# Reordering the attention heads of a three-stage layer: projections one step sooner, score products placed between attend products, batch loops written out

## What is computed

```
x = x + tanh(g0) * experts(layernorm(x), token_ids)       # 4 gated experts, each token one of them
h0 = layernorm(x)
a  = rmsnorm(h0, ln1)                                      # attention, 16 heads of width 32
q, k, v = a @ Wq.T, a @ Wk.T, a @ Wv.T
probs = softmax(mask_causal(q k^T / sqrt(32)))             # 512 x 512 for each head
mod = 0.1 * tanh(((probs v) @ Wo.T) @ A)                   # A is 512 x 16: only rank 16 of attention is used
h  = rmsnorm(h0, ln2)
gate = silu(h @ W_in.T + mod * (h @ A) @ B)
x = x + tanh(g1) * (h0 + (gate * (h @ W_up.T)) @ W_down.T) # 16 chunks of 128 of 2048
```

## Time and profile before

| | |
|---|---|
| median of 3 runs | 1061.95 us (1060.31 to 1062.95) |
| profiled execution | 1061.96 us |
| its span | 1059.8 us |
| PE busy | 1033.5 us, 98% |
| PEld busy | 853.5 us, 81% |
| DVE busy | 722.4 us, 68% |
| ACT busy | 589.6 us, 56% |
| POOL busy | 252.1 us, 24% |
| chain that ended last | PE 86%, DVE 8%, issue 3%, DMA 1%, ACT 1% |

### The profile page before, as it was taken

The page is one execution under the profiler, slowest core; times in us unless marked ns, Lnnn a source line. Parts: engine busy times, 40 slices in busy tenths (PEclk is TensorE's granted clock), DMA queues, the critical chain, the costliest instruction groups (busy, mean ns, idle before and its releaser), DMA issues.

```text
span 1059.8 us, 17623 instructions
## 1 busy us (share of the span) xinstructions
PE 1033.5 (98%) x5336; PEld 853.5 (81%) x5337; DVE 722.4 (68%) x1661; ACT 589.6 (56%) x1399; POOL 252.1 (24%) x252
## 2 busy tenths in 40 slices
PE   6999999999999999999999999999999999999998
PEld 6787878877888878878888888778888888788887
DVE  7766756996665559985665479966655599854443
ACT  4464546886434447875444368864344478753342
POOL 4536123641000115640000136410001155300000
PEclk9999999999999999999999999999999999999999
DMA  6534133443222416343322354432234253322221
GB/s 239 201 141 161 49 117 74 96 110 134 90 89 91 147 47 173 69 127 129 106 90 89 111 141 98 113 130 90 89 91 147 63 157 80 95 86 89 89 89 50
DMA packets 47084, 115.93 MB, mean 109 GB/s; under 512 B 6800, under 2 KB 6800, under 8 KB 46096
## 3 DMA queue, kind: packets, MB, share of 16 engines
q1 hardware_dynamic: 43968, 105.06, 33.2%
q0 software_dynamic: 3040, 9.96, 2.7%
HBM read 76.46 MB, written 13.37 MB: 85 GB/s over the span
## 4 chain that ended last, share of the span: by engine, by line
PE 86%; DVE 8%; issue 3%; DMA 1%; ACT 1%; SPq 0%; DVEq 0%; POOL 0%; POOLq 0%
PE bank L518 67%; PE bank L721 5%; PE bank L735 4%; DVE wr L1329 3%; PE bank L684 3%; DVE nb L1341 2%; PE bank L688 1%; PE bank L770 1%; DMA stack<-wr 1%; PE bank L574 1%; PE bank L589 1%; DVE big L1350 1%; PE bank L632 1%; SPq L312 0%; ACT wr L887 0%
## 5 line engine op out<-in xcount | busy, mean ns | idle before, releaser
L518 PE MATMUL bank<-hT,wr 128*128 128x512 f32 x1488 | 358.4, 390 | 0.0
L518 PEld LDWEIGHTS bank<-hT,wr 128*128 128x128 f32 x1488 | 278.8, 188 | 60.0 <-issue 1.3
L518 PE MATMUL bank<-wr,actr 128*128 128x512 f32 (+1 forms) x1224 | 303.1, 397 | 2.4 <-DVE actr L1311 1.5
L518 PEld LDWEIGHTS bank<-wr,actr 128*128 128x128 f32 x1224 | 228.8, 190 | 51.1 <-issue 3.3
L491 POOL TENSOR_SCALAR big<-big,rr 128x128 f32<-128x128 f32 (+1 forms) x128 | 138.9, 1094 | 131.7 <-DVE rr L1346 131.2
L1380 DVE SCALAR_TENSOR_TENSOR wr<-stream,lns,wr 128x256 fp32r<-128x256 f32 x256 | 121.7, 536 | 51.0 <-ACT wr L1006 51.0
L972 ACT ACTIVATE big<-bank,nb 128x512 f32<-128x512 f32 (+3 forms) x256 | 131.7, 527 | 27.9 <-DVE nb L1341 27.7
L430 POOL TENSOR_TENSOR wqs<-wstage,wqs 128x512 fp32r<-128x512 f32 x32 | 43.0, 1353 | 436.8 <-ACT wqs L887 435.4
L1329 DVE TENSOR_TENSOR wr<-bank,wr 128x512 fp32r<-128x512 f32 (+1 forms) x224 | 124.5, 600 | 22.2 <-ACT wr L887 22.2
L887 ACT ACTIVATE wr<-bank 128x512 fp32r<-128x512 f32 (+1 forms) x224 | 106.0, 538 | 52.9 <-PE bank L518 30.1
L887 ACT ACTIVATE actr<-act_sb 128x512 fp32r<-128x512 f32 x64 | 40.4, 632 | 145.7 <-DVE act_sb L1394 145.7
(11 more groups left out here) (180 smaller groups left out, 1039.6 us busy)
## 6 DMA issues: line engine op xcount, KB each, us to landing
stream<-in_wmlp SPq DMA_DIRECT2D x64, 512.0 KB, 4.0
stack<-wr SPq DMA_DIRECT2D x192, 128.0 KB, 2.3
stream<-in_wmlp SPq DMA_DIRECT2D x64, 256.0 KB, 2.7
big<-in_x SPq DMA_DIRECT2D x4, 1024.0 KB
big<-y_rows SPq DMA_DIRECT2D x4, 1024.0 KB, 5.5
residual<-big SPq DMA_DIRECT2D x4, 1024.0 KB
big<-residual SPq DMA_DIRECT2D x4, 1024.0 KB, 5.6
out<-big SPq DMA_DIRECT2D x3, 1024.0 KB, 4.5
```

The costliest lines, as they stand in the source:

```text
L518: mm = pe.matmul(dst, lhs(pl, k), rhs(pr, k), start=start and i == 0, stop=stop and i == n - 1, skip_group_check=skip)
```

## The change

On PE, the step of head `n` is now: turn of `n+1` in one run, the score rows of tiles 2 and 0 of head `n+3`, and then attend products of head `n` with the other short products between them; then half a projection for the step after, the two MLP products (from step 9), the last score row of head `n+4`, and the last attend product. The values are waited for ahead of the turn. Projections of groups 2 and 3 are done in the lead-in (one half) and in steps 0 to 6; all of group 1's K is in the lead-in. The tiles are turned in the order 2, 1, 3, 0, and the banks copied in the order 6, 5, 4. Normalising tile 0 goes to ACT, tile 1 to POOL. The product with zeros is gone. PE's and SP's loop over the batches is written out, that of ACT and DVE stays. SP has one more wait at the first head of groups 1 to 3; POOL makes the weights of group 2's Q in the lead-in.

```diff
-VALUES, LOW_RANK = (4, 6), 5
+VALUES, LOW_RANK = (6, 4), 5
-NORM_DVE, NORM_POOL = (3, 1), (0, 2)
+NORM_DVE, NORM_ACT, NORM_POOL = 3, 0, (1, 2)
+TURN_ORDER = (2, 1, 3, 0)
+TURNED_BANKS = ((6, 256, 1024), (5, 512, 512), (4, 512, 0))
+COPY_AT = {(0, 0): (1, 1), (0, 2): (2, 0), (1, 0): (2, 1), (1, 2): (3, 0), (2, 0): (3, 1)}
+WEIGHTS_AT = {(0, 0): (2, 1), (0, 2): (3, 0), (1, 0): (3, 1)}
+PART_OF = {2: 1, 1: 2, 3: 2, 0: 3}
...
                     sp.wait_ge(qk_lo, g * 2 + 2)
+                    if q:
+
+                        sp.wait_ge(s_done, g * (3 * QH) - 3)
...
-            with pe.Fori(0, NB - 1) as b:
-                batch(b, True)
-            batch(NB - 1, False)
+            for b in range(NB):
+                batch(b, b < NB - 1)
...
+            def project_part(b, head):
+
+                q, j = head // QH, head % QH
+                if q < NQ - 2:
+                    project(b, q + 2, j // 2, half=j % 2)
...
+                if j == 0:
+                    pe.wait_ge(vst_lo, b * NQ + q + 1)
                 if head < H - 1:
-                    turn_probs(n + 1, (j + 1) % 2)
+                    wait_probs(n + 1)
+                    for kt in TURN_ORDER:
+                        turn_tiles(n + 1, other, kt)
                 if head < H - 3:
...
+                    pe.wait_ge(exp_ok, (n + 3) * 4 - 1)
+                    score_rows(other, 2, True)
+                    score_rows(other, 0, False)
+                if head < H - 1:
+                    first, second, third, last = (0, 1, 3, 2) if head == 0 else TURN_ORDER
+                    attend(first, HI)
+                    if head < H - 3:
+                        mask(1, 2 * P, 2)
+                        pe.wait_ge(exp_ok, (n + 3) * 4)
+                        score_rows(other, 1, True)
+                        mask(2, P, 1)
+                    attend(first, LO)
+                    for kt in (second, third):
+                        attend(kt, HI)
+                        attend(kt, LO)
+                    attend(last, HI)
+                    project_part(b, head + 1)
...
+                    if head < H - 4:
+                        scores_last(n + 4, j % 2, stack_loads(b, head + 4))
+                    attend(last, LO).then_inc(pv_done, 1)
...
-                pe.matmul(bank[ATT][:, :], zeror[:, :], hT[:, HI, 0, :], start=True, stop=False,
-                          skip_group_check=True).then_inc(pv_done, 1)
...
+                project(b, 1, 1)
+
+                wait_probs(b * H)
...
-                scores(b * H + 2, 0, b * (H // 2) * 48 + 96)
-                project(b, 1, 1, half=0)
+                scores(b * H + 2, 0, stack_loads(b, 2))
+                project_part(b, 0)
+                scores_last(b * H + 3, 1, stack_loads(b, 3))
...
+            def normalise(n, par):
+                act.wait_ge(rr_ok, n + 1)
+                rows = prob_rows(par, NORM_ACT)
+                a.activation(rows, rows, ACT.Copy, scale=rr[:, par, NORM_ACT:NORM_ACT + 1]).then_inc(pn_act, 1)
...
-                for qt in NORM_DVE:
-                    rows = prob_rows(par, qt)
-                    v.tensor_scalar(rows, rows, rr[:, par, qt:qt + 1], None, ALU.mult).then_inc(pn_ok, 1)
+                rows = prob_rows(par, NORM_DVE)
+                v.tensor_scalar(rows, rows, rr[:, par, NORM_DVE:NORM_DVE + 1], None, ALU.mult).then_inc(pn_ok, 1)
```

More of the change, by code:

```diff
@@ L386, in _ @@
             sp.wait_ge(y_stored, 16 * ITEMS)
-            batch(0, True, first=True)
-            with sp.Fori(1, NB - 1) as b:
-                batch(b, True)
-            batch(NB - 1, False)
+            for b in range(NB):
+                batch(b, b < NB - 1, first=b == 0)
             sp.wait_ge(out_in, (NB - 1 + TT) * 16)
@@ L692, in scores, with mask, scores_last, scores_middle @@
+            def mask(bk, at, n):
+                pe.matmul(bank[bk][:, at:at + P * n], identr[:, :], maskr[:, 0:P * n],
+                          start=False, stop=True, skip_group_check=True).then_inc(s_done, 1)
+            def scores_last(n, par, loads, first=False):
+                pe.wait_ge(stk[par], loads)
                 if not first:
                     pe.wait_ge(exp_ok, n * 4 - 3)
-                rows(3, True)
+                score_rows(par, 3, True)
                 mask(0, 3 * P, 1)
+            def scores_middle(n, par, first=False):
@@ L726, in attend, with scores @@
-            def attend(b, q, n, j):
-                pe.wait_ge(pt_lo, n * 3 + 3)
-                pe.wait_ge(vst_lo, b * NQ + q + 1)
-                for kt in range(TT):
-                    _, _, at = TURNED[kt]
-                    w = S - kt * P
-                    for part in (HI, LO):
-                        at_row = 64 * (j // 2) + R * (j % 2)
-                        mm = pe.matmul(bank[ATT][0:3 * R, kt * P:S], vst[:, q % 2, kt, at_row:at_row + 3 * R],
-                                       pts[:, j % 2, part, at:at + w], start=False, stop=False, skip_group_check=True)
-                mm.then_inc(pv_done, 1)
+            def scores(n, par, loads, first=False):
+                scores_last(n, par, loads, first)
+                scores_middle(n, par, first)
+                scores_second(n, par, first)
@@ new lines, in turn, with turn_tiles @@
+            def turn(n, par, kt, qt):
+                bk, col, _ = TURNED[kt]
+                src = SCORE[qt][2] + kt * P
+                mm = pe.transpose(bank[bk][:, col + (qt - kt) * P:col + (qt - kt) * P + P],
+                                  prob[par][:, src:src + P], ident[:, :])
+                if qt == TT - 1 and kt != 1:
+                    mm.then_inc(p_turned, 1)
+            def turn_tiles(n, par, kt, first=False):
+                if not first and kt != 3:
+                    pe.wait_ge(pt_lo, (n - 1) * 3 + PART_OF[kt])
+                for qt in range(kt, TT):
+                    turn(n, par, kt, qt)
@@ L745, in head_step, with attend @@
-                if j == 0 and q < NQ - 1:
-                    project(b, q + 1, 1, half=1)
-                elif j and q < NQ - 2:
-                    project(b, q + 2, (0, 0, 1)[j - 1], half=(0, 1, 0)[j - 1])
+                head, other = q * QH + j, (j + 1) % 2
+                def attend(kt, part):
+                    _, _, at = TURNED[kt]
+                    at_row = 64 * (j // 2) + R * (j % 2)
+                    return pe.matmul(bank[ATT][0:3 * R, kt * P:S], vst[:, q % 2, kt, at_row:at_row + 3 * R],
+                                     pts[:, j % 2, part, at:at + S - kt * P], start=head == 0 and kt == 0 and part == HI, stop=False,
+                                     skip_group_check=True)
@@ L999, in head_step @@
                     values_high_of(b, q + 1)
+                for i, (bk, w, at) in enumerate(TURNED_BANKS):
+                    act.wait_ge(p_turned, n * 3 + i + 1)
+                    copy(pts[:, j % 2, HI, at:at + w], bank[bk][:, 0:w]).then_inc(pt_hi, 1)
+                    if i == 0 and (q < NQ - 1 or j < QH - 1):
+                        normalise(n + 1, (j + 1) % 2)
             def split_gate_up(b, c, par):
```

106 lines of the change are left out of this document (49 added, 57 removed).

## The result

| | before | after |
|---|---|---|
| median of 4 runs | 1061.35 us (1060.31 to 1062.95) | 1054.03 us (1053.56 to 1054.30) |
| profiled execution, its span | 1061.96, 1059.8 us | 1054.3, 1052.6 us |
| PE busy | 1033.5 us, 98% | 1022.9 us, 97% |
| DVE busy | 722.4 us, 68% | 702.6 us, 67% |
| ACT busy | 589.6 us, 56% | 601.6 us, 57% |

The ratio is 0.9924 (0.9911 to 0.9936): the changed kernel is faster by 7.3 us. That lies 1.9 us under the forecast of 1055.9 and inside the range. Of the 1.9, 0.6 belong to the kernel before, whose median came out at 1061.35 and not at the 1061.95 that the forecast starts from; as a difference, 7.3 us stand against 6.1.

The account below looks back on a forecast made before the run. PE was taken to limit the lead-in, early steps and MLP, DVE the later steps. Per batch 4.2 - 0.9 - 3.6 - 0.5 = -0.8, so -3.2; with loops -2.9, -6.1 from 1061.96: 1055.9 us, range 1051.0 to 1061.0.

Parts of the forecast that it names:

- Lead-in and step 0, +4.2: Start of each batch: added projections 2.78, a score row 0.29 and waiting 1.3, less 0.15: +4.2 us a batch.
- The wait: PE at head 1's turn waits for the values' low part from DVE: 1.3 us a batch, bounds 0 and 1.6.
- The zeros product: Lead-in on PE: dropping it gives back nothing, since the next score product waits 0.23 us longer for its transfer.
- Steps 1 to 6, -0.9: PE-limited steps: better placed short products save 0.15 us a step, 4.50 in place of 4.65; -0.9 us a batch.
- Steps 7 to 12, -3.6: DVE-limited steps: one scaling less takes DVE's step from 4.10 to 3.72 us; 26.50 becomes 22.89, -3.6 a batch.
- Steps 13 to 15, -0.5: Last steps: fewer scalings in the chain, against POOL's longer pair; -0.5 us a batch, between -1.0 and +0.3.
- Loop, -2.9: PE's gaps where batches 1 and 2 begin vanish with the loop written out: 2 x 1.47 = -2.9 us in all.
- Old pace in the late steps: Rival: ACT's added scaling makes ACT's queue the limit, late steps stay at 4.10 us; 1067.1 us, chance 0.09.
- Columns and loads adding up: Rival: PE's short products cost the same in any place, so their saving is lost; 1060.1 us, chance 0.06.
- Values in time: Rival: the values are ready at head 1's turn, so the 1.3 us wait is absent; 1050.7 us, chance 0.07.
- A written-out program that stalls: Rival: PE's longer list begins each batch with the old gaps, so 2.9 is not won; 1058.8 us, chance 0.08.

Follow-up runs that it names:

- the later wait: Changed kernel, with PE waiting for the values at the first attend product instead of ahead of the turn: 1049.13 us, ratio 0.9879.
- the short products back: Changed kernel, with each step's score products in one run again and all attend products behind them, ending on 128 columns: 1055.11 us, ratio 0.9932.
- The scalings alone: Kernel before, with only the new division of scalings (DVE tile 3, ACT tile 0, POOL tiles 1 and 2): 1059.7 us, ratio 0.9984.
- the projections one step later: Changed kernel, with every half projection of a later group one step later and nothing else moved: 1079.11 us, ratio 1.0167.

## Why the prediction was right, step by step

**Lead-in and step 0, +4.2.** Measured 30.76 against 26.57 in batch 3 of the kernel before: +4.19. The wait was 1.37 (1.3 taken, 1.2 from the rows). The zeros product was worth nothing, as said. That the wait is real and mostly a matter of its place, the later wait showed.

**Steps 1 to 6, -0.9.** Mis-sized: -1.4 in batch 1 (28.07 to 26.64). A PE step lost 0.18, not 0.15: three savings of 0.06. The size of all three was nearly right, but the account of the third was not. By starts the mask of tile 3 cost 0.06 in the kernel before too (424.95 to 425.01), and the 0.05 fell on the score product behind it; the prediction put it on the mask. And the mask need not stand in front of an attend product: the experiment with the short products back keeps this saving with the mask in front of transposes. Beyond 6 x 0.18 = 1.1, 0.11 of the -1.4 is an end that lies elsewhere (step 0 ends with a shorter attend product), and the rest is step 1, which was 4.83 before in batch 1 and 4.69 in batch 3. The scalings alone bring it to 4.68 in batch 1, so I take the rest as a wait for DVE.

**Steps 7 to 12, -3.6.** Measured -3.8 (26.50 to 22.68), 3.78 a step on average, and 3.72 from reciprocal to reciprocal without extra work. Size and limit were right, the cause was half told. The scalings alone give 0.5 of this a batch. Right beside DVE's 4.10 lay the ring through turn, score row and maxima at 4.15, which the old order could not leave; the 0.40 us that DVE waited for a mask in the earlier trace rows, which I took for a lead that could be used up, was a wait on one edge of that ring. The change opened it, by my reading through the new place of the score row, to which the prediction gave no term. So the sum came out as if there were no ring, and that was luck.

**Steps 13 to 15, -0.5.** Measured -0.45 in batch 1 (8.36 to 7.91) and -0.24 in batch 3 (8.19 to 7.95), with POOL's longer pair as the next limit, as feared there.

**Loop, -2.9.** Measured -3.0 between the medians of the experiment on it alone. The gaps of both jumps, 2.97 together, are gone; the traces show 1.4 us more, in batches 0 to 2 outside the gaps, for which the prediction had no term and I have no cause.

**The sum.** Batch 1 of the kernel before is longer than its batch 3, so the terms above do not simply add. Taken from batch 3 in both kernels they are 4.18 - 1.27 - 3.70 - 0.24 = -1.03. The changed kernel's last attend product has 512 columns, the other's 128, so the start by which I end a batch stands 0.17 further ahead of the real end there; that leaves -0.86, for the forecast's -0.8. Against the kernel with only its loops written out, and with this 0.17, the batches are shorter by 0.9, 1.0, 0.3 and 1.0, 3.1 us for the forecast's 3.2. Batch 2 gains less, since a score row in step 8 waits 1.01 for its transfer. The loops give 4.4 from the first attention projection on, and the stage ahead of it was 0.4 longer (161.33 for 160.94): 3.1 + 4.4 - 0.4 = 7.1, for 7.2 between the two spans. So the terms of a batch came out nearly as forecast, and what the traces show beyond the forecast stands in the batches that ran in the loop.

**The rivals.** Old pace in the late steps: not so, 3.78, and ACT did not become the limit even with twice the columns. Columns and loads adding up: ruled out by the short products put back. Values in time: they were not. A written-out program that stalls: no gap.

## What to carry to other kernels

Where an engine seems to limit a step by its own work, look for a short wait inside that step: it can be the sign of a ring between engines just as long, and then taking work off the engine gives little until the ring is opened (1.7 us here, for 6.6 with the new order). A wait for data belongs in front of the instruction that reads the data; placed ahead of a turn and two score rows that do not read the data, it cost 1 us in each batch here. Work moved in front of a wait is free only as long as the wait is there, so gains from moving work and from removing the wait do not add.

## What the runs showed of the hardware

- Ten fp32 transposes take 1.01 to 1.02 us, to the start of what follows, whether an attend product (as in the changed kernel) or a 128-column mask (419.62 to 420.64) stands in front. The row behind them costs 0.09 more than elsewhere: 512 columns 0.32 for 0.23, and the pair of 384 and 128 columns 0.32 where its columns are 0.17 and 0.06. Moving one row away from there leaves the 0.09 to the next.
- DVE's scaling of 512 columns costs 0.41 in its row, and that of 256 columns 0.38 behind it.
- In the run with the projections one step later, two waits of 1.2 us on PE close together were followed by 7 us at a mean clock of 0.56 in batch 2, and alike in batch 0, but not in batches 1 and 3 of the same execution. So a wait can cost more than its length, here 2.9 us on top.
